# A convolution, recurrence and expert kernel: the projection in pieces of 512 columns, and the recurrence's rates loaded straight into their widened copies

## The chip, the cores and the metric

The kernel runs on one core of a Trainium2 chip. The metric is the device time of one execution in microseconds (us); lower is better. Engines: PE multiplies matrices (TensorE), PEld is its loading of the stationary operand, DVE is VectorE, ACT is ScalarE, POOL is GpSimd, SP is the engine whose queue issues all DMAs of the stages described here.

## The reference, cut to what matters

The input is 16 images of 64 channels by 32x32. A convolutional LSTM stage gives x; each image is then 1024 tokens of 64 values, and goes through a state space layer (the part that matters here) and a layer of experts.

```
t = layernorm(tokens)                       # 16 x 1024 x 64
xs, z = split(t @ W_in)                     # 128 + 128 values
delta, Bv, Cv = xs @ W_delta, xs @ W_B, xs @ W_C
state = exp(delta[d] * A[d, n]) * state + delta[d] * Bv[n] * xs[d]   # d, n = 128, 128, token by token
y[d] = sum_n state[d, n] * Cv[n]
out = (y * silu(z)) @ W_out
```

(The kernel scales and places the factors of the term that enters the state in its own way; what counts below is which pieces are made, stored and loaded.)

## The kernel before, in words

Five stages run one after the other, each with its own blocks of instructions per engine and its own semaphores: the convolution, **the projection** (`build_project`), **the recurrence** (`build_scan`, called the scan stage below), the gate with the output product, and the experts.

**The projection.** It goes image by image (16 batches b), each in two chunks c of 512 tokens. Each engine runs its pieces in an order written out by hand through `pipelined` (L320): a piece marked (k, piece) works on the image that is k places behind the newest. PE makes the mean and the variance (L486, L491), then `xs` and `z` (L497, L499) into one PSUM bank each, then `delta` and `C` (L507, L509); ACT copies each out (L534, L535, L540, L541); DVE does the normalisation (L595 to L601) and the remainders. `delta` is stored to HBM as three bf16 parts (first, second, third remainder): ACT rounds, DVE subtracts, ACT rounds, DVE subtracts (L540, L609, L544, L615).

The token-major copies are made per tile of 128 tokens, 8 tiles to an image, in `move_tokens` (ACT), `tokens_enter` (DVE) and `last_token_parts` (POOL): PE multiplies a block of `xs` by three 128x128 matrices at once (L514, 384 columns), ACT copies 256 of them out (L557), DVE multiplies the other 128 in (L623), ACT rounds (L547, L548), DVE takes the remainders (L630, L632), ACT rounds those, POOL makes the third parts (L582, L584). All of this for image b is in the same place as its `delta` and `C`. The tokens are written out with each of their three parts two or three times over (8 pieces of 128 bf16, `TERMS`), because the products of the scan pair each part of one factor with those of the other.

**The scan stage.** Time is cut into 16 chunks of 63 steps and one of 16 per image; each chunk is done in 8 units of 16 channels. Per unit PE makes the exponents (`exponents`, L835) two units ahead and the entering terms (`enters`, L857) one unit ahead, ACT takes the exponential (L931) and carries the state (L946), DVE runs the recurrence (L1040), and PE contracts the unit's states of the chunk before (`contract`, L881). Buffers of what is loaded per chunk come in three sets, two of which take turns (`set_of`). SP loads each chunk in `load` (L767 to L787): the rates (L772, one DMA), the tokens (L778, one), the steps (L782, sixteen), the readout (L787, one); it waits before the tokens until the entering terms of the chunk two earlier are done. POOL then spreads the rates over four copies `wide`, each masked so that only every fourth channel is left (L997, four instructions of 512 columns), since one product of the exponents serves four channels at once. `store_y` (L789 to L794) issues four DMAs for each pair of chunks.

At the stage's start buffers are zeroed, the rates' matrix is split and sent through HBM (L757, L764), and then the first chunks are loaded.

Of the kernel before, what the change touches and what calls it, by code (L numbers as in the profile page):

```python
# [5 lines left out]
F32 = mybir.dt.float32  # L6
# [338 lines left out]
def terms_of(a):  # L345

    return SPLITS if a < SPLITS - 1 else SPLITS - 1
# [14 lines left out]
def gate_phase(nc, y_dram, z_dram, x1_dram, w_out, mean_w, identity, gate_w, gate_b, x2_dram, normed_dram, logit_dram):  # L362
# [5 lines left out]
    tokens = scratch("tokens_dram", (BATCH, LEN, TERMS * STATE), BF16)  # L368
# [10 lines left out]
def build_project(nc, x1_dram, w_in, w_delta, w_b, w_c, mean_w, readout_dram, z_dram, identity,  # L379
                  rates_dram, steps_dram, tokens_dram):  # L380


    with ExitStack() as ctx:
# [5 lines left out]
        wdelta, wc, wmean = sb("wdelta", [INNER, INNER]), sb("wc", [INNER, INNER]), sb("wmean", [128, 128])  # L389
        wtok = sb("wtok", [INNER, 3, 128])  # L390
# [4 lines left out]
        xs = [[sb(f"xs{i}{c}", [INNER, BANK]) for c in range(CHUNKS)] for i in range(2)]  # L395
        z = [[sb(f"z{i}{c}", [INNER, BANK]) for c in range(CHUNKS)] for i in range(2)]
        readout = [[sb(f"readout{i}{c}", [INNER, BANK]) for c in range(CHUNKS)] for i in range(2)]
        parts = [[sb(f"parts{i}{c}", [INNER, SPLITS, BANK], BF16) for c in range(CHUNKS)] for i in range(2)]
        rest = [[sb(f"rest{i}{c}", [INNER, BANK]) for c in range(CHUNKS)] for i in range(2)]
        both = [sb(f"both{i}", [128, 2, 128]) for i in range(2)]  # L400
        left = [sb(f"left{i}", [128, 2, 128]) for i in range(2)]
        steps = [sb(f"steps{c}", [128, TILES, SPLITS, INNER], BF16) for c in range(CHUNKS)]
        tokens = [sb(f"tokens{c}", [128, TILES, TERMS, STATE], BF16) for c in range(CHUNKS)]

        def ps(name):
            return ctx.enter_context(nc.psum_tensor(name, [128, BANK], F32))

        mean_ps, var_ps, xs_ps, z_ps, delta_ps, c_ps = (
            ps(n) for n in ("mean_ps", "var_ps", "xs_ps", "z_ps", "delta_ps", "c_ps"))
        tok_ps = [ps("tok_ps0"), ps("tok_ps1")]  # L410

        weights_in, eps_set = sem("weights_in"), sem("eps_set")
        x_in = [sem(f"x_in{i}") for i in range(2)]
        stored = [sem(f"stored{i}") for i in range(2)]
        tok_stored = [sem(f"tok_stored{c}") for c in range(CHUNKS)]
# [7 lines left out]
        tok_ready, both_ready, enter_ready, tok1_ready, left_ready, tok2_ready, tok3_ready = (  # L423
            sem("tok"), sem("both"), sem("enter"), sem("tok1"), sem("left"), sem("tok2"), sem("tok3"))
# [3 lines left out]
        block = ctx.enter_context(nc.Block())  # L428

        @block.sync  # L430
        def _(sp):
# [16 lines left out]
            def store(b, i, turn):  # L448
                for c in range(CHUNKS):
                    n = b * CHUNKS + c  # L450
                    sp.wait_ge(z_ready, START + n + 1)
                    sp.dma_start(z_dram[bass.ds(n, 1), :, :].rearrange("n p l -> (n p) l"), z[i][c][:, :]
                                 ).then_inc(stored[i], DMA)
                    sp.wait_ge(readout_ready, START + n + 1)
                    dst = readout_dram[bass.ds(b, 1), :, BANK * c:BANK * c + BANK]
                    sp.dma_start(dst.rearrange("b n l -> (b n) l"), readout[i][c][:, :]).then_inc(stored[i], DMA)
                    sp.wait_ge(part3_ready, START + n + 1)
                    for a in range(SPLITS):
                        dst = rates_dram[bass.ds(b, 1), :, SPLITS * a:SPLITS * a + terms_of(a), BANK * c:BANK * c + BANK]
                        sp.dma_start(dst.rearrange("b d e l -> (b d) e l"), parts[i][c][:, 0:terms_of(a), :]  # L460
                                     ).then_inc(stored[i], DMA)
                    sp.wait_ge(tok3_ready, START + (n + 1) * TILES)
                    for a in range(SPLITS):
                        dst = steps_dram[bass.ds(b, 1), BANK * c:BANK * c + BANK,
                                         SPLITS * INNER * a:SPLITS * INNER * a + terms_of(a) * INNER]
                        sp.dma_start(dst.rearrange("b (k t) e -> (b t) k e", t=128),
                                     steps[c][:, :, 0:terms_of(a), :].rearrange("p k e d -> p k (e d)")
                                     ).then_inc(tok_stored[c], DMA)
                    sp.dma_start(tokens_dram[bass.ds(b, 1), BANK * c:BANK * c + BANK, :].rearrange(
                        "b (k t) e -> (b t) k e", t=128), tokens[c][:, :, :, :].rearrange("p k e n -> p k (e n)")  # L470
                        ).then_inc(tok_stored[c], DMA)

            pipelined(sp, (0, load), (3, store))
            for i in range(2):
                sp.wait_ge(stored[i], START + BATCH // 2 * CHUNKS * STORES * DMA)
            for c in range(CHUNKS):
                sp.wait_ge(tok_stored[c], START + BATCH * TOK_STORES * DMA)

        @block.tensor
        def _(pe):  # L480
            pe.wait_ge(weights_in, START + WEIGHTS * DMA)

            def mean(b, i, turn):
                pe.wait_ge(x_in[i], START + (turn + 1) * CHUNKS * DMA)
# [1090 lines left out]
```

## Time and profile before

| | us |
|---|---|
| median of 3 runs (7505.5 to 7519.05) | 7508.6 |
| the profiled execution's own time | 7511.8 |
| its span, by the profiler | 7509.6 |
| projection, 1894 to 2464 us of the span | 570 |
| start of the scan stage, up to its first unit on DVE | 29 |
| scan stage, 2493 to 7162 us | 4669 |

Busy over the whole span: PE 87%, DVE 86%, ACT 62%, POOL 37%. The remaining 1894 us ahead and 348 us behind are the convolution, the gate and the experts. Read the stages one by one: the shares over the span mix stages with different limits. A row of a timeline gives the start, the length, the engine, the line, the tile written and the tiles read, how many instructions were merged (x8), and the idle time ahead of it with what ended it.

### The profile page before, as it was taken

The page shows a single profiled execution, that of the slowest core. Times are in us where ns is not written, and L with a number is a line of the kernel's source. Part 1 is how long each engine was busy: PE and PEld are TensorE (multiplying, and loading weights), DVE is VectorE, ACT ScalarE, POOL GpSimd, SP SyncE. Part 2 cuts the span into 40 slices and gives each one's busy share as a digit, 9 for nine tenths or more (in the row PEclk, how much of TensorE's full clock was granted, in tenths as well). Part 3 has the DMA queues.
Part 4 walks back from the last instruction along what each step waited for, and adds up shares of the span by engine and source line. Part 5 has one row for each costly group of instructions (what it writes and reads, how often), then busy time and mean ns, then how long its engine had stood idle before and what let it go on. Part 6 is the DMA issues. An engine that isn't in the chain of part 4 may idle for free. (4 is left out here: it accounts for less than half of the span.)

```text
span 7509.6 us, 170080 instructions
## 1 busy us (share of the span) xinstructions
PE 6514.4 (87%) x51873; PEld 4016.2 (53%) x51873; DVE 6491.9 (86%) x4454; ACT 4633.2 (62%) x10041; POOL 2796.1 (37%) x2188
## 2 busy tenths in 40 slices
PE   8999999999666688888888888888888888888867
PEld 3564547876222455555555555555555555555535
DVE  7888878887333799999999999999999999999962
ACT  7888778887455455555555555555555565555541
POOL 5555445554222433333333333333333333333300
PEclk9999999999767899999999999999999999999985
DMA  6666666666566211111111111111111111111153
GB/s 144 155 154 155 149 151 155 154 154 148 183 219 224 57 28 28 27 27 28 27 29 27 27 27 28 27 28 27 27 28 27 27 27 27 28 27 28 27 168 111
DMA packets 919116, 589.56 MB, mean 79 GB/s; under 512 B 682445, under 2 KB 807277, under 8 KB 918381
## 3 DMA queue, kind: packets, MB, share of 16 engines
q1 hardware_dynamic: 918397, 581.03, 32.3%
q8 instruction: 323, 5.29, 0.3%
q14 instruction: 396, 3.24, 0.1%
HBM read 161.99 MB, written 146.15 MB: 41 GB/s over the span
## 5 line engine op out<-in xcount | busy, mean ns | idle before, releaser
L1040 DVE TENSOR_TENSOR_SCAN states<-decay,enter_ps 128x1024 f32<-128x1024 f32 x2048 | 4463.6, 2261 | 106.3 <-ACT enter_ps L946 101.5
L857 PE MATMUL enter_ps<-s_steps,s_tokens 128*128 128x128 bf16 (+1 forms) x16384 | 2132.5, 310 | 551.4 <-DVE states L1040 525.5
L857 PEld LDWEIGHTS enter_ps<-s_steps,s_tokens 128*128 128x128 bf16 (+1 forms) x16384 | 1589.3, 129 | 1672.5 <-DVE states L1040 1608.6
L931 ACT ACTIVATE decay<-rate_ps 128x504 f32<-128x504 f32 x4096 | 2196.5, 588 | 80.6 <-PE rate_ps L835 5.6
L997 POOL TENSOR_SCALAR s_wide<-s_rates,mask 128x512 bf16<-128x512 bf16 (+1 forms) x1088 | 1619.6, 1506 | 303.9 <-PE rate_ps L835 283.0
L835 PE MATMUL rate_ps<-s_wide,s_decays 128*128 128x256 bf16 x8192 | 1323.7, 284 | 22.3 <-POOL s_wide L997 21.6
L946 ACT COPY enter_ps<-states 128x16 f32<-128x16 f32 x1920 | 363.2, 189 | 1585.8 <-PE enter_ps L857 1585.8
L243 POOL TENSOR_TENSOR entered<-gates 128x512 f32<-128x512 f32 x512 | 900.3, 1758 | 888.3 <-ACT gates L203 888.3
L881 PE MATMUL y_ps<-states,spread 128*32 128x512 f32 x8320 | 1121.1, 611 | 23.0 <-issue 23.0
L1003 POOL COPY spread<-s_readout 128x64 f32<-128x64 f32 (+1 forms) x272 | 63.6, 234 | 2675.8 <-PE y_ps L881 2675.8
L161 PE MATMUL pre<-rows,weights_left 128*32 128x512 f32 x8192 | 911.0, 595 | 36.1 <-POOL rows L236 23.8
L835 PEld LDWEIGHTS rate_ps<-s_wide,s_decays 128*128 128x128 bf16 x8192 | 895.9, 119 | 78.0 <-issue 21.9
L161 PE MATMUL pre<-rows,weights_right 128*32 128x512 f32 x8192 | 907.2, 593 | 0.0
L281 DVE TENSOR_TENSOR feat<-gates,squashed 128x512 f32<-128x512 f32 x512 | 903.5, 1765 | 1.4 <-ACT squashed L210 1.4
L161 PEld LDWEIGHTS pre<-rows,weights_left 128*32 128x32 f32 x8192 | 541.6, 109 | 381.3 <-issue 260.8
L161 PEld LDWEIGHTS pre<-rows,weights_right 128*32 128x32 f32 x8192 | 550.1, 109 | 333.5 <-issue 205.7
L203 ACT ACTIVATE gates<-pre,biases_left 128x512 f32<-128x512 f32 x1024 | 619.5, 688 | 134.8 <-PE pre L161 133.1
L203 ACT ACTIVATE gates<-pre,biases_right 128x512 f32<-128x512 f32 x1024 | 619.8, 688 | 126.0 <-PE pre L161 126.0
L266 DVE TENSOR_TENSOR forgot<-gates,cell 128x512 f32<-128x512 f32 x512 | 356.8, 697 | 259.9 <-ACT gates L203 259.9
L273 DVE TENSOR_TENSOR cell<-forgot,entered 128x512 f32<-128x512 f32 x512 | 347.7, 679 | 2.3 <-POOL entered L243 2.3
L210 ACT ACTIVATE squashed<-cell 128x512 f32<-128x512 f32 x512 | 330.8, 646 | 5.6 <-DVE cell L273 5.6
L881 PEld LDWEIGHTS y_ps<-states,spread 128*32 128x32 f32 x8320 | 165.6, 108 | 232.5 <-issue 229.1
(150 smaller groups left out, 2563.4 us busy)
## 6 DMA issues: line engine op xcount, KB each, us to landing
rows<-feat SPq DMA_DIRECT2D x1024, 132.0 KB, 2.4
rows<-feat SPq DMA_DIRECT2D x512, 128.0 KB, 2.4
s_steps<-steps_dram SPq DMA_DIRECT2D x4096, 8.0 KB
rows<-feat SPq DMA_DIRECT2D x512, 127.8 KB, 2.4
tokens_dram<-tokens SPq DMA_DIRECT2D x32, 1024.0 KB, 5.9
s_rates<-rates_dram SPq DMA_DIRECT2D x256, 128.0 KB, 2.6
s_tokens<-tokens_dram SPq DMA_DIRECT2D x256, 128.0 KB
rates_dram<-parts SPq DMA_DIRECT2D x64, 384.0 KB, 4.0
```

Of the source, the lines that this page charges most:

```text
L161: mm = pe.matmul(pre[c][32 * q:32 * q + 32, g, :], weights[side(s)][:, 32 * g:32 * g + 32], image(rows[s][:, q, :], MARGIN + CIMG * c), st ...
L203: a = act.activation(gates[k % GATE_RING][:, g, :], pre[k % CHUNKS][:, g, :], ACT.Sigmoid, bias=biases[side(k // CHUNKS)][:, g:g + 1])
L243: pool.tensor_tensor(entered[c][:, :], gates[k % GATE_RING][:, 2, :], gates[k % GATE_RING][:, 3, :], ALU.mult).then_inc(entered_ready, 1)
L266: dve.tensor_tensor(forgot[c][:, :], gates[k % GATE_RING][:, 1, :], cell[s][:, BANK * c:BANK * c + BANK], ALU.mult).then_inc(forgot_ready, 1)
L281: dve.tensor_tensor(image(feat[s][:, :], CIMG * c), gates[k % GATE_RING][:, 0, :].rearrange("p (h w) -> p h w", w=SIDE), squashed[c][:, :] ...
L835: mm = pe.matmul(rate_ps[h][:, QUAD * q:QUAD * q + QUAD, :], decays[:, g, 2 * h + q, :], wide[s][:, g, :, :], start=True, stop=True)
L857: mm = pe.matmul(out.rearrange("p h l -> p l h"), tokens[s][0:n * TERMS, k, :], steps[s][0:n * TERMS, k, 0:n, d:d + half], start=True, sto ...
L881: mm = pe.matmul(y_ps[q % 2][32 * j:32 * j + REACH, :].rearrange("p (r d) -> p d r", r=QUAD), spread[s][:, at:at + REACH], steps_of.rearra ...
L931: act.activation(decay[i][:, HEADS // 2 * h:HEADS // 2 * (h + 1), 1:], rate_ps[h][:, :, 0:n], ACT.Exp).then_inc(decay_ready, 1)
L946: act.copy(enter_ps[i][:, :, 0], start).then_inc(carried, 1)
L997: w = pool.tensor_scalar(wide[s][:, :, i, 0:n], rates[s][:, :, 0:n], mask[:, i:i + 1], None, ALU.mult)
L1040: dve.tensor_tensor_scan(out, factor, term, 0.0, ALU.mult, ALU.add).then_inc(scanned, 1)
```

## The change

In the projection, the token-major part is made a chunk (512 tokens) at a time instead of a tile at a time: twelve products of 128 columns fill three PSUM banks (`step_ps`, `own_ps`, `b_ps`), and ACT, DVE and POOL then work on 512 columns per instruction. It moves one place behind (3 instead of 2), its stores two (4). `z` and `C` share one bank. The stores of an image go out as one DMA per tensor or part. The tokens are stored once per part (3 pieces of 128, no longer 8). `wdelta`'s columns are permuted once (`by_place`), so that the channels which one copy of `wide` serves lie together in HBM.

In the scan stage, four DMAs of 32 partitions load the rates straight into their places in `wide`, which is zeroed once at the start; POOL's masks go. Their buffer is the one that PE reads, so they now wait for the exponents of the chunk two earlier. The tokens' eight pieces are loaded by eight DMAs, each into every eighth partition.

```diff
-            def move_tokens(b, i, turn):
-                for m in range(CHUNKS * TILES + 1):
...
-            pipelined(act, (1, deviation), (2, move_in), (2, move_out), (2, move_tokens))
+            def first_token_parts(c):
+                def piece(b, i, turn):
+                    n = b * CHUNKS + c
+                    act.wait_ge(tok_ready, START + n + 1)
+                    act.copy(own[c][:, :, :], tok_ps[1][:, :, :]).then_inc(own_ready, 1)
+                    act.wait_ge(tok_stored[i], START + turn * TOK_STORES * DMA)
+                    act.copy(of_chunk(steps[i], c, 0), tok_ps[0][:, :, :]).then_inc(step1_ready, 1)
+                    act.wait_ge(enters_ready, START + n + 1)
+                    act.copy(of_chunk(tokens[i], c, 0), enters[c][:, :, :]).then_inc(token1_ready, 1)
+                return piece
+
+            def second_token_parts(c):
+                def piece(b, i, turn):
+                    n = b * CHUNKS + c
+                    act.wait_ge(step_left, START + n + 1)
+                    act.copy(of_chunk(steps[i], c, 1), steps_left[c][:, :, :]).then_inc(step2_ready, 1)
+                    act.wait_ge(token_left, START + n + 1)
+                    act.copy(of_chunk(tokens[i], c, 1), enters_left[c][:, :, :]).then_inc(token2_ready, 1)
+                return piece
+
+            pipelined(act, (1, deviation), (2, move_in), (3, first_token_parts(0)), (2, move_out),
+                      (3, second_token_parts(0)), (2, second_part), (3, first_token_parts(1)), (3, second_token_parts(1)))
...
-            pipelined(pe, (1, variance), (2, project_in), (0, mean), (2, project_out))
+            pipelined(pe, (1, variance), (2, project_in), (3, turn_tokens(0)), (0, mean), (2, project_out),
+                      (3, turn_tokens(1)))
...
-            pipelined(pool, (0, squares), (2, last_token_parts))
+            pipelined(pool, (3, last_token_parts(0)), (0, squares), (3, last_token_parts(1)))
...
-            pipelined(dve, (1, normalise), (0, centre), (2, rest_of_delta), (2, third_part), (2, tokens_enter))
+            pipelined(dve, (1, normalise), (3, tokens_enter(0)), (2, rest_of_delta), (0, centre), (2, third_part),
+                      (3, tokens_enter(1)))
...
-            pipelined(sp, (0, load), (3, store))
+            pipelined(sp, (0, load), (3, store), (4, store_tokens))
...
-            src = decays_dram.rearrange("(g h) e n -> (h e) g n", g=GROUPS)
-            for q in range(QUARTERS):
-                sp.dma_start(decays[32 * q:32 * q + 32, :, q, :], src[32 * q:32 * q + 32, :, :]).then_inc(decays_in, DMA)
+            for i in range(QUAD):
+                for q in range(QUARTERS):
+                    at = 32 * i + TERMS * q
+                    src = decays_dram.rearrange("(g q i) e n -> i q e g n", q=QUARTERS, i=QUAD)[i, q, :, :, :]
+                    sp.dma_start(decays[at:at + TERMS, :, q, :], src).then_inc(decays_in, DMA)
...
-                sp.wait_ge(widened[s], SCAN0 + turn)
+                sp.wait_ge(rate_ready, halves_to(b, before(c) + 1))
                 sp.sem_inc(passed, 1)
-                src = rates_dram[bass.ds(b, 1), :, :, t0:t0 + n].rearrange("b (g h) e l -> (b h e) g l", g=GROUPS)
-                sp.dma_start(rates[s][:, :, 0:n], src).then_inc(rates_in[s], DMA)
+                for i in range(QUAD):
+                    src = rates_dram[bass.ds(b, 1), :, :, t0:t0 + n].rearrange(
+                        "b (g i q) e l -> i (b q e) g l", g=GROUPS, i=QUAD)[i, :, :, :]
+                    sp.dma_start(wide[s][32 * i:32 * i + 32, :, i, 0:n], src).then_inc(rates_in[s], DMA)
...
-                sp.dma_start(tokens[s][:, :, :], src).then_inc(enter_in[s], DMA)
+                for e in range(TERMS):
+                    a = STATE * (e // SPLITS)
+                    src = tokens_dram[bass.ds(b, 1), t0:t0 + n, a:a + STATE].rearrange("b (k t) n -> (b t) k n", t=BLOCK)
+                    sp.dma_start(tokens[s][e::TERMS, :, :], src).then_inc(enter_in[s], DMA)
...
-                pool.wait_ge(rates_in[s], SCAN0 + (turn + 1) * DMA)
-                pool.wait_ge(rate_ready, halves_to(b, before(c) + 1))
-                pool.sem_inc(passed, 1)
-                for i in range(QUAD):
-                    w = pool.tensor_scalar(wide[s][:, :, i, 0:n], rates[s][:, :, 0:n], mask[:, i:i + 1], None, ALU.mult)
-                w.then_inc(widened[s], 1)
```

How the change moves the instructions is shown at two places. POOL in the projection's loop, before, where `square` (awaited by PE's variance of the next place) comes first and the tiles' third parts behind it:

```order
L576 TENSOR_TENSOR square<-centred 128x512
L581 ISA
L582 TENSOR_TENSOR steps<-left,steps 128x128
L584 TENSOR_TENSOR tokens<-left,tokens 128x256
L581 REGISTER_ALU
```

and now, the third parts of a whole chunk (4 tiles) per instruction:

```order
L604 ISA
L605 TENSOR_TENSOR steps<-steps_left,steps 128x4x128
L607 TENSOR_TENSOR tokens<-enters_left,tokens 128x4x128
L597 REGISTER_ALU
L599 TENSOR_TENSOR square<-centred 128x512
L604 REGISTER_ALU
```

The eight pairs of an image behind `square` became one pair ahead of it and one behind it. The second place is SP's queue at the start of the scan stage, where the decay matrix and the first chunk are loaded, before:

```order
L764 DMA s_decays<-decays_dram 32x8x128 x4
L772 DMA s_rates<-rates_dram 128x8x64
L778 DMA s_tokens<-tokens_dram 128x4x128
L782 DMA s_steps<-steps_dram 8x4x128 x16
L787 DMA s_readout<-readouts_dram 128x64
```

and now:

```order
L787 DMA s_decays<-decays_dram 8x8x128 x16
L797 DMA s_wide<-rates_dram 32x8x64 x4
L804 DMA s_tokens<-tokens_dram 16x4x128 x8
L808 DMA s_steps<-steps_dram 8x4x128 x16
L813 DMA s_readout<-readouts_dram 128x64
```

A chunk takes 29 DMAs instead of 19, the decay matrix 16 instead of 4; the loop's loads, one per chunk, changed in the same way.

## Rows read from the trace of the kernel before

**Rows 1.** Stages: length, busy PE, PEld, DVE, ACT, POOL, granted clock, DMA share, GB/s.
```profile
1894.00:2464.00 570.00, 371.07 (x576) 138.21 (x576) 211.88 (x497) 299.64 (x817) 151.74 (x273) 0.71 0.64 214
2464.00:2493.00 29.00, 3.21 (x14) 2.31 (x15) 9.68 (x14) 2.89 (x6) 21.63 (x17) 0.50 0.23 49
2493.00:7162.00 4669.00, 4067.01 (x33516) 2614.90 (x33515) 4548.48 (x2176) 2722.71 (x6541) 1673.85 (x1354) 0.99 0.14 27
```

**Rows 2.** Timeline of DVE, projection: start, us, line, names, count [idle before].
```profile
2096.29 0.28 DVE L623 TENSOR_TENSOR both<-both,tok_ps 128x128 f32<-128x128 f32 x1
...
2102.39 0.29 DVE L623 TENSOR_TENSOR both<-both,tok_ps 128x128 f32<-128x128 f32 x1 [1.66 <-ACT both L557]
...
2104.74 0.29 DVE L623 TENSOR_TENSOR both<-both,tok_ps 128x128 f32<-128x128 f32 x1 [1.66 <-ACT both L557]
...
2130.49 0.28 DVE L623 TENSOR_TENSOR both<-both,tok_ps 128x128 f32<-128x128 f32 x1
```

**Rows 3.** Instruction groups, 2010 to 2410: busy, mean ns | idle before.
```profile
L599 DVE RECIPROCAL std<-std 128x512 f32<-128x512 f32 x12 | 40.2, 3352 | 16.3 <-ACT std L527 16.3
...
L609 DVE TENSOR_TENSOR rest<-delta_ps,parts 128x512 f32<-128x512 f32 x24 | 16.6, 692 | 58.5 <-ACT parts L540 41.6 <-DMA readouts_dram<-readout 16.9
...
L534 ACT COPY xs<-xs_ps 128x512 f32<-128x512 f32 x24 | 13.9, 579 | 40.6 <-PE z_ps L499 40.6
...
L576 POOL TENSOR_TENSOR square<-centred 128x512 f32<-128x512 f32 x11 | 11.4, 1039 | 69.9 <-DVE centred L595 69.9
```

**Rows 4.** Timeline of PE: projection early, projection later, gate stage.
```profile
1917.30 1.02 PE L499 MATMUL z_ps<-normed,win 128*128 128x512 f32 x2
1918.16 1.02 PE L486 MATMUL mean_ps<-px,wmean 128*128 128x512 f32 x2
...
2118.43 1.91 PE L499 MATMUL z_ps<-normed,win 128*128 128x512 f32 x2
...
7211.98 2.04 PE L1142 MATMUL turned_ps<-place,g_y 128*128 128x126 f32 x16 [0.60 <-DMA g_x<-x_dram]
```

**Rows 5.** A short stretch of the projection, columns of group 1.
```profile
2110.00:2112.00 2.00, 2.00 (x3) 0.74 (x3) 0.34 (x3) 1.59 (x5) 1.05 (x2) 0.50 1.03 318
```

**Rows 6.** DMA queue, 2010 to 2410 us: packets, MB, share of 16 engines.
```profile
q1 hardware_dynamic: 83265, 89.51, 66.9%
```

**Rows 7.** Page, part 5, convolution stage: busy, mean ns | idle before.
```profile
L243 POOL TENSOR_TENSOR entered<-gates 128x512 f32<-128x512 f32 x512 | 900.3, 1758 | 888.3 <-ACT gates L203 888.3
...
L281 DVE TENSOR_TENSOR feat<-gates,squashed 128x512 f32<-128x512 f32 x512 | 903.5, 1765 | 1.4 <-ACT squashed L210 1.4
```

**Rows 8.** Scan: DVE's timeline, its line 1040 (ns min/median/max), POOL's timeline.
```profile
3370.91 274.51 DVE L1040 TENSOR_TENSOR_SCAN states<-decay,enter_ps 128x1024 f32<-128x1024 f32 x126 [2.71 <-ACT enter_ps L946]
...
L1040 DVE TENSOR_TENSOR_SCAN states<-decay,enter_ps x47: 2260/2260/2261, 4988.8 to 5089.0; 128x1024 f32<-128x1024 f32 x47
...
5002.76 6.18 POOL L997 TENSOR_SCALAR s_wide<-s_rates,mask 128x512 bf16<-128x512 bf16 x4
```

**Rows 9.** Timeline of SP's queue in the scan stage.
```profile
3343.71 2.56 SPq L794 DMA_DIRECT2D y_rows_dram<-y_sb  x4
...
5001.13 0.38 SPq L778 DMA_DIRECT2D s_tokens<-tokens_dram  x1
5001.61 7.67 SPq L782 DMA_DIRECT2D s_steps<-steps_dram  x16
...
5027.25 3.11 SPq L794 DMA_DIRECT2D y_rows_dram<-y_sb  x4
```

**Rows 10.** Timeline of the scan stage's start.
```profile
2471.15 3.47 DVE L1018 MEMSET s_steps<- 128x4096 uint32 x1 [0.80 <-issue]
...
2478.42 1.81 SPq L764 DMA_DIRECT2D s_decays<-decays_dram  x4
...
2481.75 5.64 SPq L782 DMA_DIRECT2D s_steps<-steps_dram  x16
...
2493.45 6.64 DVE L1040 TENSOR_TENSOR_SCAN states<-decay,enter_ps 128x1024 f32<-128x1024 f32 x3 [17.77 <-ACT enter_ps L946]
```

More of the change, by code:

```diff
@@ L400, in build_project @@
[L400 to L403, printed above, removed]
+        xs = [sb(f"xs{i}", [INNER, CHUNKS, BANK]) for i in range(2)]
+        z = [sb(f"z{i}", [INNER, CHUNKS, BANK]) for i in range(2)]
+        readout = [sb(f"readout{i}", [INNER, CHUNKS, BANK]) for i in range(2)]
@@ new lines, in build_project @@
+        parts = [sb(f"parts{i}", [INNER, SPLITS, CHUNKS, BANK], BF16) for i in range(2)]
+        rest = [sb(f"rest{c}", [INNER, BANK]) for c in range(CHUNKS)]
+        own = [sb(f"own{c}", [128, TILES, INNER]) for c in range(CHUNKS)]
+        enters = [sb(f"enters{c}", [128, TILES, STATE]) for c in range(CHUNKS)]
+        enters_left = [sb(f"enters_left{c}", [128, TILES, STATE]) for c in range(CHUNKS)]
+        steps_left = [sb(f"steps_left{c}", [128, TILES, INNER]) for c in range(CHUNKS)]
+        steps = [sb(f"steps{i}", [128, CHUNKS * TILES, SPLITS, INNER], BF16) for i in range(2)]
@@ L405, in ps @@
+        tokens = [sb(f"tokens{i}", [128, CHUNKS * TILES, SPLITS, STATE], BF16) for i in range(2)]
         def ps(name):
             return ctx.enter_context(nc.psum_tensor(name, [128, BANK], F32))
[L408 to L412, printed above, removed]
+        mean_ps, var_ps, xs_ps, zc_ps, delta_ps = (ps(n) for n in ("mean_ps", "var_ps", "xs_ps", "zc_ps", "delta_ps"))
@@ L448, in store @@
             def store(b, i, turn):
[L449 to L452, printed above, removed]
-                                 ).then_inc(stored[i], DMA)
[L454 to L471, printed above, removed]
@@ L474, in _ @@
+            pipelined(sp, (0, load), (3, store), (4, store_tokens))
             for i in range(2):
-                sp.wait_ge(stored[i], START + BATCH // 2 * CHUNKS * STORES * DMA)
-            for c in range(CHUNKS):
-                sp.wait_ge(tok_stored[c], START + BATCH * TOK_STORES * DMA)
+                sp.wait_ge(stored[i], START + BATCH // 2 * STORES * DMA)
+                sp.wait_ge(tok_stored[i], START + BATCH // 2 * TOK_STORES * DMA)
         @block.tensor
@@ L542, in move_out, with second_part @@
+            def second_part(b, i, turn):
                 for c in range(CHUNKS):
                     act.wait_ge(rest1_ready, START + b * CHUNKS + c + 1)
-                    act.copy(parts[i][c][:, 1, :], rest[i][c][:, :]).then_inc(part2_ready, 1)
-            def token_parts(c, k, a, tile, ready):
-                act.copy(steps[c][:, k, a, :], tile[:, 0, :])
-                act.copy(tokens[c][:, k, SPLITS * a:SPLITS * a + SPLITS, :],
-                         tile[:, 1:2, :].broadcast_to([128, SPLITS, STATE])).then_inc(ready, 1)
@@ L678, in build_scan @@
         tokens = [sb(f"s_tokens{s}", [128, blocks[s], STATE], BF16) for s in range(SETS)]
-        rates = [sb(f"s_rates{s}", [128, GROUPS, kept[s]], BF16) for s in range(SETS)]
         wide = [sb(f"s_wide{s}", [128, GROUPS, QUAD, kept[s]], BF16) for s in range(SETS)]
@@ L702, in build_scan @@
         readout_in = [sem(f"readout_in{s}") for s in range(SETS)]
-        widened = [sem(f"widened{s}") for s in range(SETS)]
         spread_ready = [sem(f"spread_ready{s}") for s in range(SETS)]
@@ L1017, in _ @@
                 dve.memset(decay_end[i][:, :, :], 0.0)
+            for s in range(SETS):
+                dve.memset(wide[s][:, :, :, :], 0.0)
             dve.memset(steps[1][:, :, :, :], 0.0).then_inc(vector_zeroed, 1)
-            dve.wait_ge(consts_in, SCAN0 + 2 * DMA)
-            dve.tensor_reduce(mask[:, :], ident[:, :].rearrange("p (q i e) -> p i q e", i=QUAD, e=TERMS), AX.XY, ALU.add
-                              ).then_inc(mask_ready, 1)
             dve.wait_ge(rate1, SCAN0 + 1)
```

178 lines of the change are left out of this document (98 added, 80 removed).

## The prediction

> **What bounds the kernel now.** Read first the busy time by stage [rows 1]: in the projection (570 us) no engine is busy for more than 371 us, so a chain of waits sets it; in the scan stage (4669 us) DVE is busy for 4548, so DVE sets it. The two are costed apart.
>
> In the projection the timeline of DVE [rows 2] shows the chain. From one image's first tile to the next image's first tile pass 2130.49 - 2096.29 = 34.2 us, and 16 x 34.2 = 547 of the 570 us; 23 us are filling and draining. The tiles follow each other every 2.35 us, each time with DVE idle for 1.66 us behind ACT's copy: 8 tiles are 18.8 us in which ACT and DVE hand pieces of 128 to 384 columns to and fro. The other 15.4 us are variance, xs, z, delta and C. The DMA queue is busy for 66.9% [rows 6], 22.9 of 34.2 us, though in bursts: in some stretches its share is full [rows 5].
>
> In the scan stage the units' recurrences run back to back: 274.51 / 126 = 2.18 us each [rows 8].
>
> **The projection's new period.** One period is now the same work, but tokens of one image run beside delta and C of the next, in 512 columns per instruction.
> - PE: a product of 512 columns takes 0.86 us from its start to the next at full clock (1917.30 to 1918.16), and lasts 1.02; at the lower level it lasts 1.91 [rows 4]. Ten are 8.6 us. An image's 24 products of 128 columns are 48 passes, each with its own loading of weights. The nearest row is the gate stage's product of 126 columns, 128x128 weights each: 16 passes in 2.04 us, of which the last's tail is some 0.15, so 0.12 us a pass, 5.8 us. PE in all: 14.4 us at full clock, 28.8 at half.
> - ACT: 21 instructions at a step of some 0.5 us (one lasts 0.58), 10 us; DVE: the reciprocal 3.35 and 12 of 0.69, 11.6 us; POOL: 5 of 1.04 at least, 5.2 us [rows 3]. None is a bound.
> - DMA: the queue moved 89.51 MB in 400 us [rows 6], 7.65 MB an image. The tokens shrink from 8 pieces to 3, by 5 x 128 x 1024 x 2 bytes = 1.31 MB. By bytes the 22.9 us become 19.0. The same bytes go as longer runs in fewer DMAs; I cost that at nothing, as SP's fewer issues here (11 an image for 20), the bank shared by z and C (its readers are done a place earlier) and the one permuting copy at the start (128 columns).
> - The chain: the variance waits for `square`, which on POOL now stands behind two third parts. From a variance on: on PE 8 products of 512 columns (6.9) and one chunk's 24 passes (2.9), with 1.0 of waits for ACT's copy and DVE's remainder, until the second delta starts at 10.8; two more products until 12.7; ACT's copy of C and the second part of the steps until 13.8; POOL's two third parts and `square`, 3 x 1.04 = 3.1, and 1.3 for DVE's two third parts of delta beside them (below). That is 18.2 us, so the stores' 19.0 come out about equal to it.
> - The clock. In the projection it is 0.71 in the mean [rows 1]: half (0.50, 1.2 GHz) in the stretch shown [rows 5] and full (2.4 GHz) where PE had run densely before, as at 1917 us [rows 4]. In the scan stage PE is busy for 87% of the time and the clock is 0.99 [rows 1]. The new period has PE at 14.4 of 18.2 to 19.0 us, 76 to 79%, with gaps up to 2.8 us, between the two. At half clock all through, PE's work on the chain (9.8 us) doubles, and the period is 28.5. I take a quarter of the time at half clock: 18.2 + 10.3 / 4 = 20.8 us.
> - Filling and draining: 23 us before. One place more for the tokens and one more for their stores; I add 11 us, an image's own two token chunks and the last stores, so 34.
>
> Sum: 16 x 20.8 + 34 = 367 us instead of 570, 203 less. Bounds: 19.0 (or 18.2, if longer runs move faster) and 28.5 a period, 325 and 490 us.
>
> **DVE and POOL together.** In the convolution POOL's product of 512 columns takes 1.76 us and DVE's beside it, with two operands in SBUF, 1.77 [rows 7], while alone they take 1.04 and 0.69 [rows 3]: each waits out the other. DVE's two third parts, `normed` and the remainders of the tokens are of this form, POOL's five too. In the chain above one such meeting is in; the others fall where POOL is idle.
>
> The Trainium skill, page GPSIMD Engine Reference, section Specifications, says that POOL shares its SBUF interfaces with VectorE and contends with instructions of two SBUF inputs. By that rule, too, taking POOL's masks away frees nothing in the scan, as the recurrence has one of its two inputs in PSUM; the trace agrees, see the next part.
>
> **The scan stage.** POOL's masks (6.18 us per chunk of 17.4) lay beside DVE's work: 47 recurrences in a row, with and without a mask beside them, took 2260 to 2261 ns [rows 8]. So their end gives nothing: 0 us. What they covered is the way from SBUF to SBUF; the rates' DMA now has to wait for the exponents of the chunk two earlier, which end one unit before the entering terms that SP awaits anyway. Behind this wait on SP's queue stand the chunk's tokens and steps. They are due one unit ahead of their chunk, some 18 us after SP is released. Tokens and steps took 8.15 us to issue (5001.13 to 5009.28) [rows 9]; seven more DMAs at 0.48 (7.67 / 16) make 11.5, which leaves 6.5 us for their landing. Per image SP issues 17 x 19 DMAs at 0.48 and nine groups of four for y at 2.8, together 181 of the 291.8 us that an image takes (4669 / 16); 170 more make it 262, 90%. I cost this at 0, and the bounds of one DMA's price are 0.48 and 0.78, that of y's (3.11 / 4) [rows 9].
>
> At the stage's start it does cost [rows 10]. DVE zeroes `wide` ahead of the rates' matrix: 4608 bf16, 2304 words at 3.47 us / 4096 words, 2.0 us, less the mask's sum of 0.2. Then 12 more DMAs for the decay matrix at 0.45 (1.81 / 4) and 10 more for the first chunk: 9.9 us. Between the last issue (2487.39) and the first unit (2493.45) lay 6.1 us, partly for masks; I take 1.5 off. Together 10 us more; bounds 9 and 12.
>
> **The sum.** Span 7509.6 - 203 + 10 = 7317. The execution's own time is 2.2 us above its span and 3.2 above the runs' median, so the forecast is 7316 for a median: 2.6% less than 7508.6.
>
> **The rivals.**
> - *PE stays at half clock.* For it: rows 5, and the gaps that remain; against it: the scan stage's 0.99 with small gaps. Then PE's 28.8 us are the bound, 490 us in the projection, 7439 in all.
> - *DVE and POOL meet each time.* All five of DVE's such instructions wait, at 1.07 more each; four are new on the chain, 4.1 us a period: 16 x 4.1 = 66, 7382. Against it: POOL is idle for two thirds of the period.
> - *SP becomes the scan's bound (slower).* If the 170 added DMAs of an image cost over (291.8 - 181) / 170 = 0.65 us each, SP's queue is slower than DVE and every chunk waits for its loads; from 0.73 on that eats the whole gain. At y's 0.78 the image takes 181 + 133 = 314 us, 22 more, times 15: 330 us, so 7646. For it: the tokens' DMAs write every eighth partition, as y's read every fourth, and y's are the dearest on the queue. Against it: the steps' sixteen small ones, 0.48. The Trainium skill, page DMA: Bandwidth & Descriptors, section Rules for kernel authors, speaks for this rival: small transfers should be coalesced into one, and under 64 KB one pays mostly overhead; the change does the reverse, from one of 128 KB to four of 32 and eight of 16. By the rows that overhead is paid in parallel, off SP's queue.
> - *The change doesn't do what it says.* The half on GpSimd's masks already counts as nothing here.
>
> **How the numbers follow.** The forecast has 0.75, half clock 0.12, the meetings 0.05, SP 0.08. Of SP's case a quarter stays near the old time. A change within 0.2% (15 us) is about what the runs can't tell from none. Faster 0.92, same 0.02, slower 0.06. The range runs from the fast period with 325 us (7316 - 42 = 7274, and a little less) to the half clock's 7439; it leaves out SP's case and some of both tails.
>
> **What would show it.** In the profile after: the projection's stage near 367 us, with a period of 19 to 22 and a granted clock of 0.8 or more; L529's passes at 0.12; the DMA share there at 0.85 or more; DVE's recurrences still at 2260 ns with the same short stop between images, and SP idle before its waits for the entering terms; the start of the scan some 39 us instead of 29. Wrong it would be if SP's queue never waits in the scan, or if the clock in the projection is near 0.5.

## The result, and the profile after

The changed kernel takes 7629.5 us (median; 7621.6 to 7640.8), the kernel before 7508.7 in the same job: a ratio of 1.016, 95% interval 1.015 to 1.018. It is slower by 1.6%, where 2.6% faster was forecast. What happened is the rival that I gave 0.08: SP becomes the scan's bound. It was worked out there as 7646 us; that this lies so near is in part luck, as is said under "Why the prediction was wrong".

The profiled execution after has a span of 7638.9 us, 129.3 more than before. The stages, in the columns of [rows 1]:

```profile
1894.00:2244.00 350.00, 259.15 (x1088) 154.88 (x1088) 193.70 (x209) 191.12 (x337) 101.33 (x81) 0.89 0.84 288
2244.00:2283.00 39.00, 3.88 (x17) 2.82 (x18) 12.04 (x17) 3.39 (x7) 13.77 (x11) 0.50 0.15 31
2282.00:7297.00 5015.00, 4161.87 (x33523) 2700.62 (x33525) 4569.92 (x2176) 2723.40 (x6541) 63.77 (x271) 0.96 0.13 26
```

The projection fell from 570 to 350 us, more than the 203 us forecast. The scan's start took 39 us for 29, as forecast. The scan stage itself grew. Counted from the start of the first recurrence to the end of the last, it is 7296.4 - 2282.7 = 5014 us after and 7162.4 - 2493.5 = 4669 before. The three differences: the first recurrence starts 210.7 us earlier, the scan stage is 344.8 longer, and what follows is 4.7 shorter. Together +129.4.

DVE's recurrences hardly got slower: one takes 2264 ns in the mean for 2261. What grew is the idle time ahead of them. Page, part 5 (busy, mean ns | idle before and its releaser), and two stops on DVE's timeline, the first of them at an image's end:

```profile
L1058 DVE TENSOR_TENSOR_SCAN states<-decay,enter_ps 128x1024 f32<-128x1024 f32 x2048 | 4484.6, 2264 | 435.2 <-ACT enter_ps L972 433.4
...
3526.81 2.29 DVE L1058 TENSOR_TENSOR_SCAN states<-decay,enter_ps 128x1024 f32<-128x1024 f32 x1 [9.25 <-ACT enter_ps L972]
3531.31 2.29 DVE L1058 TENSOR_TENSOR_SCAN states<-decay,enter_ps 128x1024 f32<-128x1024 f32 x1 [2.21 <-ACT enter_ps L972]
```

That line names ACT's carry, and the carry waits for PE's entering terms. What these waited for in the scan stage is in the list of PE's waits (waited for: us in total, times, longest):

```profile
PE enter_ps L883 <- DMA s_steps<-steps_dram: 342.8, 137, 8.3
```

In the kernel before this list has no wait for a load. So the loads come too late, by 343 us in all, and the stage is 345 us longer. The stop at an image's end was 2.7 us in [rows 8], and the group in the kernel before read:

```profile
L1040 DVE TENSOR_TENSOR_SCAN states<-decay,enter_ps 128x1024 f32<-128x1024 f32 x2048 | 4463.6, 2261 | 106.3 <-ACT enter_ps L946 101.5 <-ACT decay L931 4.6
```

Next the timeline of SP's queue in the stage:

```profile
3380.71 1.82 SPq L797 DMA_DIRECT2D s_wide<-rates_dram  x4
3382.85 5.35 SPq L804 DMA_DIRECT2D s_tokens<-tokens_dram  x8
3388.39 7.66 SPq L808 DMA_DIRECT2D s_steps<-steps_dram  x16
3396.36 0.36 SPq L813 DMA_DIRECT2D s_readout<-readouts_dram  x1
3397.04 3.01 SPq L820 DMA_DIRECT2D y_rows_dram<-y_sb  x4
3400.39 2.73 SPq L797 DMA_DIRECT2D s_wide<-rates_dram  x4
3403.45 5.45 SPq L804 DMA_DIRECT2D s_tokens<-tokens_dram  x8
3409.08 7.44 SPq L808 DMA_DIRECT2D s_steps<-steps_dram  x16
3416.77 0.36 SPq L813 DMA_DIRECT2D s_readout<-readouts_dram  x1
```

There is no gap of more than 0.4 us in these 36 us: SP issues all the time. Eight tokens DMAs take 5.4 us, 0.67 to 0.68 each, and the four rates DMAs 1.8 to 2.7. Sixteen steps DMAs still take 7.4 to 7.7, as in [rows 9]. The waits of SP's queue in the whole scan stage say the same. Before:

```profile
SPq L775 <- PE enter_ps L857: 1538.4, 239, 16.7
SPq L791 <- ACT y_sb L954: 73.5, 17, 23.3
```

After:

```profile
SPq L793 <- PE rate_ps L861: 29.6, 15, 3.7
SPq L817 <- ACT y_sb L980: 18.5, 1, 18.5
```

A queue that waits has slack, that is, time in which it could issue more. Before it was 1612 us, 100.7 per image. After it is 48.

### The profile page after: what moved, and what is told of

The parts are those of the page before. It is cut to its first block and busy times, and to the rows that moved or that the text cites. A ratio compares the mean times of both kernels' runs of the same rounds, so it can differ in the third digit from the quotient of the medians.

```text
span 7638.9 us, 174643 instructions
## 1 busy us (share of the span) xinstructions
PE 6495.3 (85%) x52385; PEld 4033.3 (53%) x52385; DVE 6495.1 (85%) x4169; ACT 4526.7 (59%) x9561; POOL 1127.3 (15%) x908
## 5 line engine op out<-in xcount | busy, mean ns | idle before, releaser
L1058 DVE TENSOR_TENSOR_SCAN states<-decay,enter_ps 128x1024 f32<-128x1024 f32 x2048 | 4484.6, 2264 | 435.2 <-ACT enter_ps L972 433.4
L883 PE MATMUL enter_ps<-s_steps,s_tokens 128*128 128x128 bf16 (+1 forms) x16384 | 2203.3, 317 | 834.3 <-DVE states L1058 464.5
L883 PEld LDWEIGHTS enter_ps<-s_steps,s_tokens 128*128 128x128 bf16 (+1 forms) x16384 | 1659.7, 133 | 1936.4 <-DVE states L1058 1515.1
L861 PE MATMUL rate_ps<-s_wide,s_decays 128*128 128x256 bf16 x8192 | 1366.7, 290 | 21.6 <-DMA s_wide<-rates_dram 20.9
L161 PEld LDWEIGHTS pre<-rows,weights_left 128*32 128x32 f32 x8192 | 500.6, 109 | 423.1 <-issue 182.8
L161 PEld LDWEIGHTS pre<-rows,weights_right 128*32 128x32 f32 x8192 | 505.9, 109 | 377.0 <-issue 141.1
L972 ACT COPY enter_ps<-none 128x16 f32<-128x16 f32 x128 | 22.5, 176 | 256.7 <-PE enter_ps L883 256.6
```

The lines of the kernel that those rows point to most:

```text
L161: mm = pe.matmul(pre[c][32 * q:32 * q + 32, g, :], weights[side(s)][:, 32 * g:32 * g + 32], image(rows[s][:, q, :], MARGIN + CIMG * c), st ...
L861: mm = pe.matmul(rate_ps[h][:, QUAD * q:QUAD * q + QUAD, :], decays[:, g, 2 * h + q, :], wide[s][:, g, :, :], start=True, stop=True)
L883: mm = pe.matmul(out.rearrange("p h l -> p l h"), tokens[s][0:n * TERMS, k, :], steps[s][0:n * TERMS, k, 0:n, d:d + half], start=True, sto ...
L972: act.copy(enter_ps[i][:, :, 0], start).then_inc(carried, 1)
L1058: dve.tensor_tensor_scan(out, factor, term, 0.0, ALU.mult, ALU.add).then_inc(scanned, 1)
```

## The experiments

Three theories:
1. **SP's issuing time bounds the scan.** Its queue takes longer per image than DVE does.
2. **The rates land late.** They now go into the tile that the exponents read, behind the wait for the exponents of two chunks ago, with no second buffer.
3. **The small transfers crowd each other on the DMA engines**, whoever issues them.

Each scan stage below is counted from the first recurrence's start to the last one's end in the run's own profile.

### Undoing the halves

**e1_scan_before**: the new projection, with the rates' one DMA and GpSimd's masks back, and the tokens loaded by one DMA (and so stored eight times over, as before):

```diff
-    for e in range(TERMS):
-        ... sp.dma_start(tokens[s][e::TERMS, :, :], src)
+    src = tokens_dram[bass.ds(b, 1), t0:t0 + n, :].rearrange("b (k t) (e n) -> (b t e) k n", t=BLOCK, e=TERMS)
+    sp.dma_start(tokens[s][:, :, :], src).then_inc(enter_in[s], DMA)
-    for i in range(QUAD):
-        ... sp.dma_start(wide[s][32 * i:32 * i + 32, :, i, 0:n], src)
+    sp.dma_start(rates[s][:, :, 0:n], src).then_inc(rates_in[s], DMA)
```

> The new projection with the recurrence's loads and masks of before (one rates DMA, GpSimd's masks, one tokens DMA; so the tokens are stored eight times again, by 11 stores instead of 4). Theory 1, SP's queue is the new bound of the scan stage: the scan stage returns to 4669 us. The projection has 1.31 MB more to store per image, 3.9 us of queue time for each of 16 images, so some 410 us instead of 350. Sum about 7629 - 340 + 60 = 7350. Theory 2 (the rates now wait for the exponents and land late) and theory 3 (the small transfers crowd each other on the DMA engines) expect the same here; this run measures what the projection alone is worth.

**e2_masks_back**: only the second half of that diff, so the tokens keep their eight DMAs.

> Only the rates go back to one DMA and GpSimd's masks; the eight tokens DMAs stay. Theory 1: a chunk costs SP 17.1 - 3.0 + 0.7 = 14.8 us, an image 17 x 14.8 + 9 x 3.35 = 282 us, under DVE's 292: the whole loss is back, scan stage 4669, total about 7290. Theory 2: also everything is back, 7290. Theory 3: the tokens' eight transfers stay, so the scan stage stays over 4800, total over 7400.

**e3_tokens_one**: only the first half, so the rates keep their four.

> Only the tokens go back to one DMA (stored eight times, 11 stores an image); the rates stay at four DMAs straight into the widened copies, behind the wait for the exponents. Theory 1: a chunk costs SP 17.1 - 5.6 + 0.5 = 12.0 us, an image 234 us: scan stage 4669, projection some 60 us longer than in the changed kernel, total about 7350. Theory 2: the rates are as late as before, the scan stage stays at 5008, total about 7690. So neither half of the edit alone would cost anything by theory 1, though both together cost 340 us.

Measured: e1 7355.2 us, e2 7338.4, e3 7358.9; ratios to before 0.980 (0.978 to 0.982), 0.978 (0.976 to 0.979) and 0.980 (0.978 to 0.982). The scan stage is 4639, 4708 and 4643 us. Undoing either half takes nearly the whole 345 us away; so neither costs it alone. Theory 2 falls with e3 (the rates still land behind the wait), theory 3 with e2 (the tokens' transfers stayed). What each half takes from the queue is all that they share. e2 missed its expectation, 7290, by 48 us: its stage is 39 us longer than that of before. Its queue is the fullest of the three (282 us an image by the sum in the expectation), and its PE still waits for the steps' loads, 50.2 us in 25 stops; in e1 and e3 it never does. DVE's recurrences, full-size, in e1 and in e2 (busy, mean ns | idle before):

```profile
L1068 DVE TENSOR_TENSOR_SCAN states<-decay,enter_ps 128x1024 f32<-128x1024 f32 x2048 | 4463.0, 2261 | 80.1 <-ACT enter_ps L974 75.0 <-ACT decay L959 4.9
```

```profile
L1068 DVE TENSOR_TENSOR_SCAN states<-decay,enter_ps 128x1024 f32<-128x1024 f32 x2048 | 4467.2, 2262 | 142.2 <-ACT enter_ps L974 136.6 <-ACT decay L959 4.8
```

e1 and e3 also show what the smaller token store is worth: with the tokens stored eight times, by eleven DMAs instead of four, the first recurrence starts 88 us later than in the changed kernel (86 in e3). The period there comes to 24 to 27 us, and DMA's share in the middle of the stage is full, 1.02 (columns of [rows 1], e1):

```profile
1960.00:2200.00 240.00, 179.55 (x675) 101.81 (x674) 120.86 (x129) 118.44 (x208) 64.33 (x50) 0.83 1.02 303
```

### Moving the issues to another queue

**e4_rates_act**: all transfers stay, and ACT issues the rates' four, one per unit:

```diff
 (ACT, unit)
     decays_of(*following(b, u + 1))
+    if g >= GROUPS - 2:
+        load_next(b, c, g - GROUPS + 2, first, ending)
+    if g < 2:
+        load_next(b, c - 1, g + 2, first, ending)
```

> All transfers of the changed kernel as they are, but the four rates DMAs of a chunk are issued by ACT, one in each of four units, behind the exponential that says that the old rates are used up. Theory 1: SP's chunk costs 14.0 us, an image 268 us, under 292: scan stage 4669 or a little more, total about 7290, faster than both kernels. The risk is ACT's own time: an issue of 0.5 us before the next carry may delay DVE, at most 4 x 0.5 us a chunk, 288 us in all, then 7570. Theory 3 (crowding on the DMA engines): nothing changes, 7630.

**e9_y_act**: all loads stay on SP in their order, and ACT issues y's four stores:

```diff
 (ACT, unit)
     decays_of(*following(b, u + 1))
+    if g < QUAD:
+        if c in (0, 1) and not first:
+            store_y(b - 1, SHEETS - 2 + c, [g])
+        if c % 2 and c > 1:
+            store_y(b, (c - 1) // 2 - 1, [g])
```

> The changed kernel with all its loads as they are on SP's queue, in the same order and behind the same waits; only the four stores of y of each group are issued by ACT, one in each of the four units after its copy. If only the time that SP's queue takes counts: SP's image is 313.4 - 9 x 3.3 = 284 us, under DVE's 292, and the scan stage falls from 5014 to about 4720 (as with the masks back, where the queue was nearly as full): total about 7340. If what is slow is the rates' DMAs landing in the tile that the exponents read, or the wait ahead of them, nothing changes: 7630.

**e10_rates_gpsimd**: the rates' four are issued by GpSimd where the masks stood (`pool.dma_start(wide[...])`).

> As the run with the rates on ACT's queue, but the four rates DMAs of a chunk are issued by GpSimd, which is idle since the masks went, at the place where the masks stood. By SP's relief alone the scan stage is 4640 to 4660 and the total 7280 to 7300. What no trace here shows is the price of a DMA that GpSimd issues: up to 4 us each it stays hidden (a chunk takes 17.4 us). Against it: if DVE and GpSimd keep each other waiting while it writes the descriptors, the recurrence's 2260 ns grow.

Measured: e4 7286.8 us (ratio 0.971, 0.969 to 0.972), e9 7348.4 (0.979, 0.977 to 0.980), e10 7304.8 (0.972, 0.971 to 0.974). Scan stages 4652, 4713 and 4672 us; e10's is 12 us over its expectation. e9 is the sharpest of them: it touches neither the rates nor the tokens nor their own waits, and it takes 301 of the 345 us away, because SP has four DMAs less to issue for every pair of chunks. (The wait for y's copy leaves SP's queue too, but it had held SP up only once, for 18.5 us.) Theory 2 expected nothing of e9, and theory 3 nothing of e4 and, as all transfers stay, nothing of e9 either. e4 is the fastest kernel of the study, 3% faster than before and 4.5% faster than the changed one. Its queues, SP's and ACT's, whose issues (0.32 us) lie beside its exponentials, and the wait that SP has again:

```profile
3396.39 3.44 SPq L814 DMA_DIRECT2D y_rows_dram<-y_sb  x4
3400.17 5.46 SPq L798 DMA_DIRECT2D s_tokens<-tokens_dram  x8
3405.81 7.64 SPq L802 DMA_DIRECT2D s_steps<-steps_dram  x16
...
3380.25 0.59 ACT L951 ACTIVATE decay<-rate_ps 128x504 f32<-128x504 f32 x1
3380.60 0.32 ACTq L963 DMA_DIRECT2D s_wide<-rates_dram  x1
3380.74 0.59 ACT L951 ACTIVATE decay<-rate_ps 128x504 f32<-128x504 f32 x1
...
SPq L794 <- PE enter_ps L877: 285.7, 137, 5.9
```

### Number, stride and filling of the queue

These add DMAs to the kernel before, with nothing of the change in it:

```diff
+    for t in range(10):
+        src = steps_dram[bass.ds(b, 1), t0 + t:t0 + n:BLOCK, :].rearrange("b k (e d) -> e (b k) d", e=TERMS)
+        sp.dma_start(again[s][TERMS * t:TERMS * t + TERMS, :, :], src).then_inc(enter_in[s], DMA)
     sp.wait_ge(spread_ready[s], SCAN0 + turn)
```

**e5_add10** is this. **e6_add10_strided** has `again[s][t::BLOCK, :, :]` in its place. **e7_add16** is e5 with `range(16)`.

> The kernel before with ten more DMAs per chunk on SP's queue: ten of the steps' own loads issued a second time into a spare tile of the same partitions, 8 neighbouring partitions each. 170 more issues an image, the same number as the change adds, but of the cheap form: 0.475 us each as the steps' sixteen take 7.6. Theory 1a (what counts is the number times the price, and these are cheap): SP's image is 181 + 170 x 0.475 = 262 us, still under 292: no loss, 7509. Theory 1b (at 90% filling of the queue the loads are already late, whatever their price): a part of the loss appears, some 50 to 150 us.

> As the run with ten more DMAs, with one difference: each of the ten writes every sixteenth partition of the spare tile instead of 8 neighbouring ones (bytes, shape and source are the same). In the trace of the changed kernel the DMAs that write or read every eighth or fourth partition (tokens 557 ns, y 542) take SP twice as long as those on neighbouring partitions (steps 278, rates 317). If the stride makes that, each costs 0.67 instead of 0.475: SP's image is 181 + 170 x 0.67 = 295 us, just over 292, and the whole some 50 to 100 us over the kernel before, 7560 to 7610. If the price has another cause (bytes or rows of the source), it is as the run before.

> The kernel before with sixteen more cheap DMAs per chunk. Theory 1: SP's image is 181 + 272 x 0.475 = 310 us, 18 over the 292: 15 x 18 = 275 us more, 7785, with nothing of the change in it. If SP's issues are not what bounds the scan stage, 7509.

**e8_contiguous** is the changed kernel with

```diff
-    sp.dma_start(tokens[s][e::TERMS, :, :], src).then_inc(enter_in[s], DMA)
+    sp.dma_start(tokens[s][BLOCK * e:BLOCK * e + BLOCK, :, :], src).then_inc(enter_in[s], DMA)
```

> The changed kernel with each tokens DMA writing 16 neighbouring partitions instead of every eighth; number, bytes and sources of all DMAs as they are. The tokens then meet the wrong steps, so this run computes another sum in the entering terms; the work is the same. If the stride is what makes these DMAs dear, eight of them take 3.8 us instead of 5.4, SP's image 315 - 17 x 1.6 = 288 us, just under 292, and the scan stage falls from 5014 to 4670 to 4740: total 7290 to 7360. If the stride costs nothing: 7630.

Measured: e5 7514.0 us (ratio 1.0005, 0.9995 to 1.0014), e6 7991.6 (1.064, 1.063 to 1.066), e7 7678.0 (1.023, 1.021 to 1.025), e8 7317.4 (0.974, 0.973 to 0.976). Scan stages 4670, 5145, 4839 and 4681 us.

e5 adds exactly the 170 DMAs an image of the change, at the price on which my prediction rested or less, and nothing is lost: that part of the forecast was right. e6 adds the same number, the same bytes and the same sources with another stride of partitions, and the kernel is 6.4% slower. The two lines of the trace, e5's and e6's (count: ns min/median/max), and SP's timeline in the same order:

```profile
L788 SPq DMA_DIRECT2D again<-steps_dram x2720: 273/278/1484, 2486.7 to 7139.2; - x195
...
3394.40 3.62 SPq L788 DMA_DIRECT2D again<-steps_dram  x10
```

```profile
L788 SPq DMA_DIRECT2D again<-steps_dram x2720: 563/621/1515, 2488.8 to 7624.0; - x195
...
3390.18 7.19 SPq L788 DMA_DIRECT2D again<-steps_dram  x10
```

So a DMA whose tile has neighbouring partitions takes SP 0.28 us, 0.36 from one to the next, and one with every sixteenth partition 0.62 and 0.72. (The steps' own sixteen, of the same form, also take 278 ns each, but 0.48 from one to the next; the last part says more of this.) e8 shows it in the changed kernel from the other side: eight tokens DMAs take 3.7 us instead of 5.4, and 333 of the 345 us are gone. Its timeline, and the line of the tokens' DMAs:

```profile
3388.97 3.68 SPq L804 DMA_DIRECT2D s_tokens<-tokens_dram  x8
3392.83 7.21 SPq L808 DMA_DIRECT2D s_steps<-steps_dram  x16
...
L804 SPq DMA_DIRECT2D s_tokens<-tokens_dram x2176: 315/375/1888, 2274.9 to 6940.0; - x198
```

In the changed kernel the same line reads

```profile
L804 SPq DMA_DIRECT2D s_tokens<-tokens_dram x2176: 495/557/1696, 2268.6 to 7269.1; - x198
```

The filling follows from the waits. DVE's image takes 291.8 us and SP waited for 100.7 of them. For each run the image's growth and these 100.7 us, over the number added, give the price of one DMA: e7 (302.4 - 291.8 + 100.7) / 272 = 0.41 us, e6 (321.5 - 291.8 + 100.7) / 170 = 0.77, the change (313.4 - 291.8 + 100.7) / 170 = 0.72. In e7, e6 and the change SP still waits for 3 to 4 us an image, which these prices contain; without them they are 0.40, 0.75 and 0.70. In e5 the queue has much more to wait:

```profile
SPq L776 <- PE enter_ps L863: 504.0, 197, 7.8
```

That is 31.5 us per image, so that its DMAs took (100.7 - 31.5) / 170 = 0.41. In e6 and e7 it is PE again that waits for the last loads of the chunk:

```profile
PE enter_ps L863 <- DMA again<-steps_dram: 429.6, 150, 7.2
```

```profile
PE enter_ps L863 <- DMA again<-steps_dram: 153.0, 70, 6.7
```

The loss does not begin only when the queue is full. Where SP still waits for 31.5 us an image (e5), PE never waits for a load; with 18 to 19 us (e4, e10) PE waits for 5 and 22 us over the stage, with 10 to 13 us (e2, e8, e9) for 46 to 54, and with 3 us (the changed kernel) for 343. For e6 I had expected 50 to 100 us and got 482: I had taken 0.67 a DMA and 181 us for the rest, and both were too low. For e7 I had expected 7785 with 0.475 a DMA, too much.

### What bounds the projection now

**e11_less_stored**: the changed kernel with the steps stored in three pieces:

```diff
     for a in range(SPLITS):
-        dst = steps_dram[bass.ds(b, 1), :, SPLITS * INNER * a:SPLITS * INNER * a + terms_of(a) * INNER]
-        ... steps[i][:, :, 0:terms_of(a), :].rearrange("p k e d -> p k (e d)")
+        dst = steps_dram[bass.ds(b, 1), :, INNER * a:INNER * a + INNER]
+        ... steps[i][:, :, a, :]
```

> The changed kernel with the steps stored in three pieces instead of eight (the recurrence then reads the first for all eight, so the entering terms are another sum; number and shape of its loads stay). 1.31 MB less is stored per image, the same amount that the tokens lost in the change. Theory A, the chain of products and copies sets the projection's 18.5 to 20 us a period, as forecast (18.2 against the stores' 19.0): 350 us fall to 335 or stay. Theory B, the stores set it: the two runs with the tokens stored eight times took 88 us more for 1.31 MB an image, so 16 x 4 to 5.5 us fall away, 350 becomes 262 to 290. The scan stage stays at 5014 in both; total 7615 to 7630 by A, 7540 to 7570 by B.

Measured: 7628.1 us (ratio 1.016, 1.014 to 1.017), and the first recurrence at 2282.8 us, where the changed kernel has it at 2282.7. The middle of the projection, first in the changed kernel and then in e11 (columns of [rows 1]):

```profile
1960.00:2200.00 240.00, 191.94 (x842) 115.72 (x840) 149.46 (x162) 147.06 (x261) 79.99 (x63) 0.94 0.93 321
```

```profile
1960.00:2200.00 240.00, 193.31 (x840) 116.43 (x839) 148.00 (x161) 145.70 (x259) 79.96 (x62) 0.94 0.75 249
```

The DMA share falls from 0.93 to 0.75 and the engines' work in the stretch stays: the chain sets the period (theory A), with the stores close behind. With 1.31 MB more, in e1 and e3, they take over. Those two runs also store in more and smaller DMAs; what the bytes and what their number cost is not separated.

## Why the prediction was wrong, point by point

- **The projection's period: right in kind, a little pessimistic.** From the third image's reciprocal to the last one's pass 2182.96 - 1927.61 = 255.4 us, 13 periods of 19.6:

```profile
1927.61 3.35 DVE L626 RECIPROCAL std<-std 128x512 f32<-128x512 f32 x1 [0.97 <-ACT std L544]
...
2182.96 3.35 DVE L626 RECIPROCAL std<-std 128x512 f32<-128x512 f32 x1 [1.27 <-ACT std L544]
```

  Forecast were 20.8, of which 18.2 for the bare chain and 2.6 for a quarter of the time at half clock. The granted clock was 0.89 in the stage and 0.94 in its middle, against 0.71 before, so this term was too large: by the same sum 0.94 is an eighth of the time at half clock, 1.2 us, which gives 19.4. (The 28.5 us at half clock do not come out of their own terms: 18.2 + 9.8 is 28.0, and PE's whole work is 28.8. And four meetings at 1.07 are 4.3 us, not 4.1. Neither moves the forecast by more than 2 us.) Filling and draining are 350 - 16 x 19.6 = 36 us for 34.
- **"About equal" for chain and stores: right**, by e11 on one side and by e1 and e3 on the other.
- **PE's pass of 0.12 us** [rows 4]: 24 passes of a chunk took 2.68 us, 0.11 each, in PE's timeline from the first of its twelve products to the product behind them:

```profile
2048.42 0.38 PE L529 MATMUL step_ps<-wtok,xs 128*128 128x128 f32 x2
...
2051.10 1.02 PE L493 MATMUL mean_ps<-px,wmean 128*128 128x512 f32 x2
```

- **DVE and POOL together.** One meeting on the chain was counted, and it is there: DVE's third parts take 1.18 us in the mean for 0.69, POOL's `square` 1.49 and its third part of the tokens 1.39 for 1.04 (groups from 1960 to 2200 us):

```profile
L607 POOL TENSOR_TENSOR tokens<-enters_left,tokens 128x512 bf16<-128x512 f32 x25 | 34.7, 1388 | 0.0
...
L640 DVE TENSOR_TENSOR parts<-rest,parts 128x512 bf16<-128x512 f32 x26 | 29.6, 1175 | 15.3 <-ACT parts L567 15.3
...
L599 POOL TENSOR_TENSOR square<-centred 128x512 f32<-128x512 f32 x12 | 17.8, 1485 | 0.0
```

- **The start of the scan, 39 us: right** (38.6 from the first memset to the first recurrence).
- **Masks at nothing: right.** In e1 the recurrence takes 2261 ns with the masks, and in the changed kernel 2264 without any.
- **The step that failed: the scan stage's steady part, "I cost this at 0".** It is a sum over SP's queue, with two terms too small. The price of an added DMA was taken as 0.48, from the steps' sixteen [rows 9], and is 0.72. Seven of the ten write with a stride, and the row with their form was y's, 0.78, which reads with one. And the queue without them was put at 181 us per image and was 291.8 - 100.7 = 191: in the timeline of before the DMAs alone take some 172 us an image, less than I took, but what lies between their groups had been left out. So the queue came to 191 + 122 = 313 us, not 262, and as DVE's image takes 291.8, each image grew by 21.6 us. The 122 are that growth and the slack, so this sum is no check by itself; the rows of the timeline above are one: the tokens' group takes 5.4 us for 0.4 before and the rates' 2.3 in the mean for 0.4, 17 x 6.9 = 117 us an image. The bound "0.65 us each" was really 100.7 / 170 = 0.59, and the upper end of my own range for the price was on the wrong side of it by far. My own sign of being wrong, that SP's queue never waits, came true but for 16 waits.
- **The rival** had the mechanism and the place. Its argument for it, the stride, is what e6 and e8 showed. That its size fits (314 us an image; 313 measured) is luck: its price for a DMA, 0.78, was too high and its 181 us for the rest too low, by 10 us each. The other row of y's in [rows 9] gives 2.56 / 4 = 0.64, and with that the rival would have forecast no loss. Its total of 7646 is near 7629.5 also because the projection gained some 18 us more than it had been given. I gave it 0.08 on the ground that sixteen small DMAs cost 0.48, which only says what small DMAs cost, not strided ones. The price range 0.48 to 0.78 had its threshold inside; 0.08 was no fair chance for it, and the range of the forecast should have reached over 7646.
- **The Trainium skill's rule**, page DMA: Bandwidth & Descriptors, section Rules for kernel authors, to coalesce small transfers, pointed the right way. By these runs the size is not what counts on SP's queue: a DMA of 8 KB with a stride takes 0.62 us, one of 16 KB without 0.38, one of 32 KB without 0.32, and the tokens' one of 128 KB before took 0.38. One large DMA is cheap there because it is one. The Trainium skill says in the same section that spreading DMAs over SP, ACT and GpSimd for bandwidth doesn't help and only saves issue time. Here issue time was the bound, and e4 shows what that is worth: 343 us.

Open: e1's and e3's scan stages are 26 to 30 us shorter than that of before, with the same loads or more. DVE's stops behind ACT's carry are fewer (in e1 22 with 75.0 us, before 28 with 101.5); the cause is not known. Why a strided tile costs SP more is not shown either, only that it does.

## What to carry to other kernels

Before adding DMAs to a queue, read its waits: their sum, over the number of DMAs to be added, is the price that each may have, and it contains everything between the issues. Take that price from the row with the same access form; a DMA whose tile side steps over partitions took SP 1.5 to 2.2 times as long as one with neighbouring partitions. Leave some slack: here PE began to wait for loads when SP's waits fell below some 20 us of an image's 292. And when a queue is full, the cheapest mend may be another queue: the changed kernel with four of its DMAs per chunk issued by ACT is 3% faster than before, while as written it is 1.6% slower.

## What the runs showed of the hardware that I had not expected

- The number of issues and the bytes alike, a partition stride in the SBUF tile raised SP's time for a DMA from 278 to 621 ns (e5, e6), and for the tokens' from 375 to 557 (e8, after).
- GpSimd issued the rates' four DMAs in 2.4 us (e10), against 1.8 to 2.7 on SP, though one takes it 582 ns and SP 317, with the recurrence beside them at 2261 ns as before:

```profile
3386.22 2.40 POOL L1019 DMA_DIRECT2D s_wide<-rates_dram  x4 [0.54 <-issue]
...
s_wide<-rates_dram POOLq DMA_DIRECT2D x1024, 32.0 KB, 2.2
```

  They landed 2.2 us after issue, against 1.8 from SP.
- The steps' sixteen DMAs took SP 7.5 us in the loop over the images and 5.6 us in the last image, which stands behind the loop, though one DMA takes 278 ns in it and 301 behind it (medians). Kernel before:

```profile
6864.70 7.52 SPq L782 DMA_DIRECT2D s_steps<-steps_dram  x16
...
6978.43 5.56 SPq L782 DMA_DIRECT2D s_steps<-steps_dram  x16
```

  In the loop SP executes two register operations, of 29 and 37 ns, with nearly each of them (4080 and 3825 in the trace, for 4352 DMAs), and behind it none; that is about half of the difference, and the rest is not explained. An estimate from these rows: the difference comes to 17 x 1.95 = 33 us of SP's image, more than the 21.6 that the change lost per image. No run tried to save them.
